# Attention scores, maxima, exponentials and transposes handled by pairs of heads instead of by tiles of tokens

## The reference

```
q  = layernorm(x) @ Wq         # 16 query heads of 16, in 4 groups per key head
k, v = ctx @ Wk, ctx @ Wv      # 4 key heads of 16
q, k = rope(q), rope(k)
scores = sum over groups g of q[g] . k         # [batch, 4 heads, 256, 120]
attn   = softmax(scores / 4);  out = mean over heads of (attn @ v)
x1 = x + tanh(g_xattn) * out @ Wo
# mixture of experts on layernorm(x1): gate softmax, top 2 of 8 experts, renormalised
x2 = x1 + tanh(g_ffn) * sum over the two chosen e of w_e * (silu(g_e) * u_e) @ down_e
```

## Time and profile before

| what | value |
|---|---|
| median of 3 runs | 455.38 us (455.07 to 457.28) |
| the profiled execution | 455.58 us, its span 453.7 us |
| busy over the span | PE 405.6 us (89%), DVE 217.9 (48%), ACT 204.9 (45%), POOL 263.3 (58%) |
| mean granted PE clock | 0.956 of full speed |
| first matmul of the expert stage (L965) | 111.58 us |

### The profile page before, as it was taken

One profiled execution on the slowest core, in us unless ns is written; L12 is line 12 of the kernel. 1 busy time (PEld: TensorE's weight loads), 2 busy tenths in 40 slices (PEclk: granted clock), 3 DMA queues, 4 the chain that ended last, 5 costly groups with the idle time before them and its releaser, 6 DMA issues.

```text
span 453.7 us, 10880 instructions
## 1 busy us (share of the span) xinstructions
PE 405.6 (89%) x2470; PEld 339.4 (75%) x2471; DVE 217.9 (48%) x579; ACT 204.9 (45%) x453; POOL 263.3 (58%) x266
## 2 busy tenths in 40 slices
PE   6977787638999999999999999999999999999940
PEld 6644464424788888888898888988889888888840
DVE  2555998856534434344443344443444434444330
ACT  1569966221563246336435622563347336433210
POOL 3116879784387239936954972398229936953221
PEclk9998996956999999999999999999999999999995
DMA  8960024911036114531632461146213541112111
GB/s 274 402 250 25 23 96 140 304 49 49 25 116 210 38 24 107 171 94 24 208 117 45 136 189 24 24 120 206 46 24 83 166 123 24 24 24 37 37 28 12
DMA packets 19624, 46.68 MB, mean 103 GB/s; under 512 B 2368, under 2 KB 13760, under 8 KB 16512
## 3 DMA queue, kind: packets, MB, share of 16 engines
q1 hardware_dynamic: 11632, 35.20, 22.4%
q0 software_dynamic: 6720, 9.64, 11.5%
q10 hardware_dynamic: 1248, 1.57, 1.0%
HBM read 37.67 MB, written 9.00 MB: 103 GB/s over the span
## 4 chain that ended last, share of the span: by engine, by line
PE 76%; DVE 7%; POOL 5%; ACT 3%; DMA 3%; issue 3%; POOLq 1%; SPq 0%; DVEq 0%; ACTq 0%
PE att L985 21%; PE sc L965 20%; PE misc L965 10%; PE qbank L965 10%; PE pT L975 6%; POOL dn L459 2%; DMA x<-in_x 2%; PE att L949 2%; ACT gu L614 1%; PE sc L783 1%; PE att L765 1%; DVE stats L1049 1%; PE qbank L790 1%; PE sc L803 1%; DMA out<-xT_all,index_out 1%
## 5 line engine op out<-in xcount | busy, mean ns | idle before, releaser
L507 POOL DMA_INDIRECT out<-xT_all,index_out x34 | 54.6, 1604 | 110.0 <-DVE xT_all L1371 106.3
L985 PE MATMUL att<-dn,hT 128*128 x816 | 114.1, 289 | 1.0 <-DVE hT L1349 1.0
L985 PEld LDWEIGHTS att<-dn,hT 128*128 128x128 f32 x816 | 101.6, 190 | 1.3 <-issue 1.2
L965 PE MATMUL sc<-gu,xT 128*128 x408 | 102.5, 400 | 0.0
L965 PEld LDWEIGHTS sc<-gu,xT 128*128 128x128 f32 x408 | 74.1, 188 | 14.8
L965 PE MATMUL misc<-gu,xT 128*128 x204 | 80.0, 392 | 1.5 <-ACT xT L687 0.8
L965 PE MATMUL qbank<-gu,xT 128*128 x204 | 80.0, 392 | 0.0
L393 POOL TENSOR_TENSOR gu<-wraw,gu 128x2048 f32 x14 | 64.5, 4622 | 9.4 <-ACT gu L603 7.3
L1345 DVE TENSOR_TENSOR xT_all<-xT_all,sc 128x512 f32<-128x512 f32 x34 | 23.4, 688 | 87.6 <-ACT xT_all L694 87.6
L694 ACT ACTIVATE xT_all<-misc 128x512 f32<-128x512 f32 x34 | 20.3, 598 | 75.8 <-PE qbank L965 72.5
L1345 DVE TENSOR_TENSOR xT_all<-xT_all,qbank 128x512 f32<-128x512 f32 x34 | 23.4, 688 | 60.7 <-ACT xT_all L694 60.7
(11 more groups left out here) (161 smaller groups left out, 488.0 us busy)
## 6 DMA issues: line engine op xcount, KB each, us to landing
wraw<-in_gu SPq DMA_DIRECT2D x16, 1024.0 KB, 5.4
wraw<-in_dn SPq DMA_DIRECT2D x8, 1024.0 KB, 5.1
x<-in_x SPq DMA_DIRECT2D x8, 266.0 KB, 12.2
xT_all<-in_xT SPq DMA_DIRECT2D x4, 512.0 KB, 11.7
out<-x SPq DMA_DIRECT2D x8, 256.0 KB, 2.2
rows_scratch<-x SPq DMA_DIRECT2D x3, 532.0 KB, 3.9
xT_all<-rows_scratch,index_in POOLq DMA_INDIRECT x37, 2.9
out<-xT_all,index_out POOLq DMA_INDIRECT x34, 3.9
```

Of the source, the lines that this page charges most:

```text
L507: nc.gpsimd.indirect_dma_start(out=out_d, out_offset=bass.IndirectOffsetOnAxis(ap=index, axis=0), in_=y[:, r, :], in_offset=None, compute_ ...
L965: mm = nc.tensor.matmul(bank[2 * hf + n][:, :], xT[:, par, xp, k, :], gu_part(where, wp, k * 2 * I + col, HALF), start=(k == 0 and xp == 0 ...
L985: mm = nc.tensor.matmul(bank[6][:, 0:D], hT[:, hf, hp, j * P:(j + 1) * P], dn_part(where, wp, (hf * JH + j) * D, D), start=(hf == 0 and j ...
```

## The change

Scores, maxima, exponentials, transposes and copies of a batch are cut the other way: by pair q of heads, over both tiles of tokens, instead of by tile j over all four heads. A pair is one bank of `sc` and one bank of `pT`. `scores(b, q)` waits only for the exponentials of pair q of the batch before; `softmax_shift(b, q)` makes four maxima instead of eight. The number of matmuls, exponentials and copies is the same; there are two reductions and two shifts per batch instead of one.

The orders of the queues change with it. On ACT, `copy_shares(t)` moves between the exponentials of the pairs, and `second_odds` from between the copies to behind the exponentials. On PE, `scores(t+1, 1)` comes behind `transpose_probs(t, 1)`. On DVE, `spread_shares(t)` moves between the two shifts, `ranks_of_picks` to the head of the turn, `first_moments(t+3)` and `mark_slots` to its end. POOL's and SP's queues are not changed.

```diff
-            def exponentials(b, j):
-                act.wait_ge(shift_ready, TB * b + j + 1)
+            def exponentials(b, q):
+                act.wait_ge(shift_ready, PAIR * b + q + 1)
                 if b >= 2:
-                    act.wait_ge(pT_psum, TB * (b - 2) + j + 1)
+                    act.wait_ge(pT_psum, PAIR * (b - 2) + q + 1)
                     act.wait_ge(spread_ready, b - 1)
-                t = TB * b + j
-                for hh in range(KVH):
+                for j in range(TB):
+                    t = TB * b + j
+                    for i in range(PAIR):
+                        hh = PAIR * q + i
...
             for t in range(B + 1):
                 if t < B:
                     copy_pT(t, 0)
+                if t < B:
+                    copy_pT(t, 1)
+                if t + 1 < B:
+                    exponentials(t + 1, 0)
+                if t < B:
+                    copy_shares(t)
+                if t + 1 < B:
+                    exponentials(t + 1, 1)
                 if t - 2 in ENDS:
                     second_odds(ENDS[t - 2])
-                if t < B:
-                    copy_pT(t, 1)
-                    copy_shares(t)
-                if t + 1 < B:
-                    exponentials(t + 1, 0)
-                    exponentials(t + 1, 1)
...
-            def scores(b):
+            def scores(b, q):
...
                 if b >= 1:
-                    pe.wait_ge(exp_done, TB * b)
+                    pe.wait_ge(exp_done, PAIR * (b - 1) + q + 1)
...
-            def transpose_probs(b, j):
-                pe.wait_ge(exp_done, TB * b + j + 1)
+            def transpose_probs(b, q):
+                pe.wait_ge(exp_done, PAIR * b + q + 1)
...
                 if t < B:
                     transpose_probs(t, 0)
                 if t + 1 < B:
-                    scores(t + 1)
+                    scores(t + 1, 0)
                 if t < B and t - 2 in ENDS:
                     ranks(ENDS[t - 2])
...
                     transpose_probs(t, 1)
+                if t + 1 < B:
+                    scores(t + 1, 1)
...
             for t in range(B + 1):
                 ranked = ENDS.get(t - 2)
-                if t < B:
-                    spread_shares(t)
                 if ranked is not None:
                     ranks_of_picks(ranked)
                 if t + 1 < B:
-                    softmax_shift(t + 1)
+                    softmax_shift(t + 1, 0)
+                if t < B:
+                    spread_shares(t)
+                if t + 1 < B:
+                    softmax_shift(t + 1, 1)
...
-                elif t + 3 < B:
-                    first_moments(t + 3)
-                if ranked is not None:
-                    for b in SETS[ranked]:
-                        mark_slots(b)
                 if t >= 1:
                     best_two(t - 1)
...
                     if t < B:
                         logit_gap(ENDS[t - 1])
+                if ranked is not None:
+                    for b in SETS[ranked]:
+                        mark_slots(b)
                 if t >= 1:
                     second_moments(t - 1)
+                    if t + 3 < B:
+                        first_moments(t + 3)
```

More of the change, by code:

```diff
@@ L234, in build_program, with score_ps @@
         o_ps, rden_ps = misc[:, 0:S], misc[:, S:2 * S]
-        def score_ps(j, hh):
-            at = (PAIR * j + hh % PAIR) * A
-            return sc[:, hh // PAIR, at:at + A]
+        def score_ps(j, q, i):
+            at = (PAIR * j + i) * A
+            return sc[:, q, at:at + A]
         inv_ps = att[:, 0, INV_AT:INV_AT + BEGINS]
@@ L604, in split_high, with copy_pT @@
                                      ACT.Copy).then_inc(w_hi, 1)
[L606 to L607 removed]
+            def exponentials(b, q):
+                act.wait_ge(shift_ready, PAIR * b + q + 1)
                 if b >= 2:
[L609 removed]
+                    act.wait_ge(pT_psum, PAIR * (b - 2) + q + 1)
                     act.wait_ge(spread_ready, b - 1)
[L611 to L616 removed]
+                for j in range(TB):
+                    t = TB * b + j
+                    for i in range(PAIR):
+                        hh = PAIR * q + i
+                        ins = nc.scalar.activation(probs[:, b % 2, j, hh, :], score_ps(j, q, i), ACT.Exp,
+                                                   bias=shift[:, q, j, i:i + 1], scale=rs[:, t:t + 1],
+                                                   accum_out=den_of[:, b % 2, j, hh:hh + 1])
                 ins.then_inc(exp_done, 1)
[L619 to L620 removed]
+            def copy_pT(b, q):
+                act.wait_ge(pT_psum, PAIR * b + q + 1)
                 if b >= 1:
                     act.wait_ge(o_psum, b)
[L623 removed]
+                nc.scalar.activation(probsT[:, PAIR * q:PAIR * (q + 1), :], pT[0:A, q, :].rearrange("a (h s) -> a h s", h=PAIR),
                                      ACT.Copy).then_inc(pT_copied, 1)
@@ L798, in scores @@
                 if b >= 1:
-                    pe.wait_ge(exp_done, TB * b)
+                    pe.wait_ge(exp_done, PAIR * (b - 1) + q + 1)
+                rows = slice(HR * PAIR * q, HR * PAIR * (q + 1))
                 for j in range(TB):
[L801 to L804, removed]
+                    mm = nc.tensor.matmul(sc[:, q, PAIR * A * j:PAIR * A * (j + 1)], qrot[rows, b % 2, P * j:P * (j + 1)],
+                                          kbd[rows, b, :, :].rearrange("p h a -> p (h a)"), start=True, stop=True)
                 mm.then_inc(s_psum, 1)
-            def transpose_probs(b, j):
-                pe.wait_ge(exp_done, TB * b + j + 1)
+            def transpose_probs(b, q):
+                pe.wait_ge(exp_done, PAIR * b + q + 1)
                 if b >= 1:
-                    pe.wait_ge(pT_copied, TB * (b - 1) + j + 1)
-                for hh in range(KVH):
-                    mm = nc.tensor.transpose(pT[0:A, j, P * hh:P * (hh + 1)], probs[:, b % 2, j, hh, :], ident)
+                    pe.wait_ge(pT_copied, PAIR * (b - 1) + q + 1)
+                for i in range(PAIR):
+                    for j in range(TB):
+                        at = S * i + P * j
+                        mm = nc.tensor.transpose(pT[0:A, q, at:at + P], probs[:, b % 2, j, PAIR * q + i, :], ident)
                 mm.then_inc(pT_psum, 1)
@@ L898, in _ @@
             mm.then_inc(wog_psum, 1)
-            scores(0)
+            for q in range(PAIR):
+                scores(0, q)
             project_keys(1, att[:, 0, :], att[:, 1, :])
@@ L1006, in step @@
                     contract(s - 1, 1, e_before)
-            pe.wait_ge(pT_copied, TB * B)
+            pe.wait_ge(pT_copied, PAIR * B)
             stay_warm(4)
@@ L1075, in rotate_q, with softmax_shift @@
                 if b >= 2:
-                    dve.wait_ge(s_psum, b - 1)
+                    dve.wait_ge(s_psum, PAIR * (b - 1))
                 V.tensor_tensor(qrot[:, b % 2, :], qbank[:, S * (b % 2):S * (b % 2 + 1)], c("rope"), ALU.mult)\
                  .then_inc(qrot_ready, 1)
-            def softmax_shift(b):
-                dve.wait_ge(s_psum, b + 1)
+            def softmax_shift(b, q):
+                dve.wait_ge(s_psum, PAIR * b + q + 1)
                 if b >= 1:
[L1083 to L1086, removed]
+                    dve.wait_ge(exp_done, PAIR * (b - 1) + q + 1)
+                link(V.tensor_reduce(negmax[:, q, :, :].rearrange("p j h -> p (j h)"),
+                                     sc[:, q, 0:KVH * A].rearrange("p (n a) -> p n a", a=A), AX.X, ALU.max, negate=True))
                 dve.wait_ge(rs_ready, b + 1)
-                V.tensor_tensor(shift[:, :, :, :], negmax[:, :, :, :],
-                                rs[:, TB * b:TB * (b + 1)].rearrange("p (q j h) -> p q j h", q=1, h=1)
-                                .broadcast_to([P, PAIR, TB, PAIR]), ALU.mult).then_inc(shift_ready, TB)
+                V.tensor_tensor(shift[:, q, :, :], negmax[:, q, :, :],
+                                rs[:, TB * b:TB * (b + 1)].rearrange("p (j h) -> p j h", h=1)
+                                .broadcast_to([P, TB, PAIR]), ALU.mult).then_inc(shift_ready, 1)
             def normalise_o(b):
@@ L1241, in _ @@
              .then_inc(wo_ready, 1)
-            softmax_shift(0)
+            for q in range(PAIR):
+                softmax_shift(0, q)
             rotate_q(1)
```

6 lines of the change are left out of this document (3 added, 3 removed).

## The result

The changed kernel takes 464.22 us (462.22 to 465.73, 4 runs) beside 455.27 for the kernel before, timed with it (4 runs, so not the 455.38 of the first three): a ratio of 1.0201, interval 1.0168 to 1.0234. It is 9 us slower; I had forecast 458.0, with 460.8 as the upper end of the range. The profiled execution took 463.89 us, its span 462.0 against 453.7; the mean granted clock is 0.949 against 0.956. The first matmul of the expert stage is at 120.17 instead of 111.58, 8.59 later, and the span grew by 8.3: all of it arises ahead of that stage, in the pipeline that the change edits.

What follows compares the result with a forecast made beforehand. The release of POOL's work was taken to bound the stage before the experts. Its second norm of set 2 +2.5 late, tail unchanged, on 455.58 gave 458.1; the median 0.2 lower, rounded up, 458.0; range 454.6 to 460.8.

Steps and rivals of the forecast that it cites:

- Turns 0 to 2: Pipeline start: ACT's gain is given back through copy_shares; normalise_o(2) at 48.0, against 48.05 before.
- E(3,0): Exponentials of batch 3, pair 0, on ACT: forecast to start at 44.7 instead of 46.01.
- T(2,1): Transposes of batch 2, pair 1, on PE: their copy was forecast to end at 44.7.
- The end of turn 2: On DVE: added first_moments(5) ends at 51.7, POOL's scale takes 1.5, so shift(4,0) not before 53.3.
- The moved odds: ACT to POOL: odds end at 58.15; POOL starts 4.65 late, absorbs 3.95, leaving at least +0.7.
- Turns 3 and 4: On DVE: moments end at 68.0; POOL waits for first_moments(7) until 68.1; second_norm(2) free at 84.9.
- Turns 5 and 6: On DVE: ends at 85.5; POOL's second norm of set 2 is +2.2 to +2.8 late, taken as +2.5.
- the rule that I had weighed: DVE marks and POOL split exclude each other; if they miss, 1.9 and 1.0 saved, sum about +1.4.
- The tail: POOL's last stretch, from second_norm of set 2 to the last mark: 20.6 us, forecast unchanged.
- rival 3: PE's clock falls in the new waits: two stretches on the way cost about 3, 460.5; chance 0.15.
- 1: Rival: POOL absorbs most of it, +0.7 to +1.4, median 456.4; chance 0.25.
- 2: Rival: ACT sets the pace without waiting for DVE, -2.9, median 452.5; chance 0.10.

Runs made afterwards that it cites:

- b3: Kernel before with only second_odds moved behind the exponentials: 454.37 us, ratio 0.9999.
- r2: Changed kernel with second_odds back between the two copies: 463.99 us, ratio 1.0200 to the kernel before.
- b2: Kernel before with only first_moments(t+3) moved to the end of the turn: 457.64 us, ratio 1.0059.
- r1: Changed kernel with first_moments(t+3) back ahead of best_two: 459.49 us, ratio 1.0112 to the kernel before.
- w1: Changed kernel with dummy matmuls of 512 columns put into PE's waits: 460.98 us, ratio 1.0134 to the kernel before.
- s2: Kernel before with its one maximum and one shift per batch made as two each, by pair, back to back: 456.36 us, ratio 1.0036.
- u2: Changed kernel with both pairs' scores together between the two transposes and first_moments back ahead of best_two: 458.07 us, ratio 1.0075.
- s1: Changed kernel with first_moments back ahead of best_two and spread_shares(t) back at the head of DVE's turn: 458.12 us, ratio 1.0084.
- p1: Changed kernel with first_moments ahead of best_two, second_odds between the copies and copy_shares ahead of the exponentials again: 458.95 us, ratio 1.0088.
- r3: Changed kernel with copy_shares(t) back ahead of both pairs' exponentials: 464.32 us, ratio 1.0188 to the kernel before.
- b1: Kernel before with a batch's four score matmuls issued by pair instead of alternating: 454.90 us, ratio 1.0009.

## Why the prediction was wrong

The direction was right, the size was not: +2.5 forecast, +9 measured. By its steps:

1. **Turns 0 to 2.** Right: `mix_values(1)` at 38.29 (I had 38.16), the gain of ACT given back through `copy_shares`. Too early: E(3,0) at 45.62, not 44.7. I took 0.6 for the scores of a pair; they took 1.08, and T(2,1) and its copy stand behind them. The half maximum was near (0.66 with a slot of 0.69; I had 0.75). `normalise_o(2)` came at 49.59, not 48.0. Of this 0.9 are of the late E(3,0). For the rest, `transpose_shares` waited 0.93 for DVE's spread copy, which took 1.14 instead of 0.23 beside POOL's split, and `attend` and `mix_values` stand behind it.
2. **The end of turn 2.** The mechanism was right, every row of it: moments, scale, shift. The shift of pair 0 began at 54.91 instead of 53.3, 1.6 late, just by what `normalise_o(2)` was late.
3. **The moved odds.** This is the step that failed: "POOL starts its long stretch 4.65 late and has 3.95 to absorb it". Odds ended at 59.69 (I had 58.15), `share_out` began at 59.84; that much was near. But it costs nothing alone (b3) and its undoing gives nothing (r2, and its POOL rows). I had POOL's slack as a fixed sum from the trace of before. It is what is left between two arrivals from DVE, and it grew in step with DVE's delay: with late moments POOL had time for late odds. In its place the runs show the moments at the turn's end, which delay DVE itself (2.6 us alone in b2, 4.7 undone in r1), and in part on the same way the clock in PE's new waits, which my sum had at nothing (3.2 in w1).
4. **Turns 3 and 4.** `first_moments(7)` ended at 71.1, not 68.0: 1.6 from step 2, 1.1 behind `attend` and `mix_values(3)` at half clock (`normalise_o(3)` at 59.52, I had 56.8), and about 0.4 more, since the marks took 1.56 (I had 1.27) and ACT's copies waited for PE behind `project_q`. I let POOL's lateness hide the added moments. With r1 (-4.7 in the changed kernel) and b2 (+2.6 alone) they are the largest single part. By the trace they act through DVE, and POOL comes in only by its answer with the scale (0.81 us at the shift, in turns 3 and 5).
5. **Turns 5 and 6.** The meeting of marks and split was brief (marks from 79.25, the split until 79.70): the marks took 1.77 where I had 3.26, the split 4.96. By the rule that I had weighed this makes the sum about 1 us smaller, and DVE did get 1.5 back. The clock took more. `normalise_o(5)` began 5.9 us after E(6,0) at 72.99, where I had 4.0, and `normalise_o(6)` 4.7 us after E(7,0), where I had 3.2; in both PE's windows are low (0.62 and 0.59). So `second_norm(2)` began 17.4 us after E(6,0) instead of the 15.3 I had. The two rows of DVE:

```profile
78.92 0.41 DVE L1103 TENSOR_TENSOR oT<-misc,rdenT 128x256 f32<-128x256 f32 x1
...
87.41 0.42 DVE L1103 TENSOR_TENSOR oT<-misc,rdenT 128x256 f32<-128x256 f32 x1 [0.83 <-PE misc L838]
```

6. **The tail**: 21.8 for 20.6, as POOL waited once for odds (0.98) and once for moments (0.39).

From the rows: 3.1 at `first_moments(7)`, 2.0 more at `second_norm(2)`, 1.2 in the tail, together 6.3 on top of the 2.5. By the runs, the mis-sized terms are the moments (at nothing beyond the 0.88 that each takes; 2.6 alone) and the clock (nothing in the sum, about 3 us in rival 3; 3.2 in w1, on a way that it shares with the moments), then the scores of a pair (1.07, not 0.6). The doubled maxima cost 1.6 in s2. A half maximum with its slot of 0.69 lies near the lower of my two bounds, 0.67, so it is not a maximum that was mis-sized.

Of the rivals, 3 happened at about its price; 1 and 2 did not: POOL absorbed the odds, but there was more than that to absorb, and ACT waited for DVE at the start of turns 3, 5 and 6.

What stays open: u2 has moments and scores back and is still 3.1 us over the kernel before. The doubled maxima cost 1.6 in s2; how the rest divides among `copy_shares` between the pairs, `spread_shares` and the later marks is within the intervals, and s1, p1 and r3 do not separate it. Undoing the odds together with u2's edits was not tried. `mark_slots` at the turn's end was never undone or moved alone.

## What to carry to other kernels

Slack that an engine shows in a trace is not a reserve: it moves with whoever feeds that engine, so ask of a moved step which loop it lies on, and time it alone in the old frame and undone in the new one before a sum is built on it. An instruction moved to the end of a turn stands ahead of the next turn's first wait. Here ACT, DVE and PE all paid for it there (2.18, 0.81 and 2.23 us), and PE's clock fell behind its wait. Work split by halves loses what the halves had by running side by side: here 1.07 us of PE per batch.

## What the runs showed of the hardware that I had not expected

- Matmuls over two halves of 64 partitions ran in twos (eight records in 1.08 us), in either loop order (b1: 1.09), as long as only score matmuls stood between them. With four transposes over 128 partitions between, four records took 1.07. For batch 0 of the changed kernel the code issues all four records of pair 0 first, and still three of pair 1 start before the last of pair 0 (13.357, seventh of eight).
- A DVE copy of 128x128 with one input took 1.14 us at 45.73, while POOL ran its split (four instructions from 41.84 to 46.78), and 0.23 us at 55.25. The Trainium skill (SBUF — State Buffer, "Who interferes with whom") has an exclusive lock on a pair of ports that DVE shares with GpSimd, and names copies among the instructions that can take it. The row agrees: not only the marks with two inputs, which I had looked at the earlier trace rows, can meet the split.
- Waits of PE of 2.2 to 2.3 us were each followed by a stretch at half clock (windows of 4 to 6 us with a mean of 0.57 to 0.72), and a few matmuls into a bank that is not in use kept it at 1.00, for 3.2 us. The length of the wait alone does not tell: a wait of 1.41 us ahead of 83.14 was followed by 0.59 from 84 to 88, and in u2 one of 1.98 us ahead of 46.78 by 1.00.
